# Two thirds of a mixture-of-experts stage sent through two experts by placed rows, the last block left as it was

## The chip, the core and the metric

The kernel runs on one core of a Trainium2 chip. The metric is the time of one execution in microseconds (us), a median over runs. The core has five engines that work side by side and are joined by semaphores: TensorE (PE in the profile; PEld is its weight load), VectorE (DVE), ScalarE (ACT), GpSimd (POOL) and SyncE (SP), which here only issues DMAs.

## The reference

A gated cross attention is followed by a mixture of experts. 1024 rows x of 128 values attend to 6404 context rows of 96 values. Then each row gets eight router weights, of which the two greatest are kept and scaled to sum to one, and eight experts (128 to 512, ReLU, 512 to 128) are summed with these weights.

```
x = x + tanh(g_xattn[0]) * xattn(layernorm(x), ctx_768, Wq, bq, Wk, bk, Wv, bv)
...
logits = einsum('bsd,de->bse', input_emb, Wr) + br          # input_emb = layernorm(x)
route_w = softmax(logits)
_, topk_idx = top_k(route_w, 2)
mask = one_hot(topk_idx, 8).sum(-2)
routed = route_w * mask
routed = routed / routed.sum(axis=-1, keepdims=True)
h = relu(einsum('bsd,edh->ebsh', input_emb, W1) + b1)
expert_out = einsum('ebsh,ehd->ebsd', h, W2) + b2
out = x + tanh(g_ffn[0]) * einsum('bse,ebsd->bsd', routed, expert_out)
```

For six of the eight experts a row's weight is zero, so what they make of it is multiplied by zero.

## The kernel before

All products that decide the result are made from a rounded value and its remainder (names ending in _hi and _lo): hi by hi, hi by lo and lo by hi, three matmuls for one product.

**Attention.** The rows are cut into tiles of 128 and into NB = 3 blocks of 2, 3 and 3 tiles. For each block a loop runs over UNITS = 26 units of two context chunks of 128 keys. In a unit TensorE makes the scores (`scores`, L943 to L945, six matmuls of 384 columns), ScalarE the exponentials, twice (L580 and L581), VectorE the remainder `ex_lo` (L751), and TensorE, LAG = 2 units later, the sum over values (`values`, L965 to L967). Score banks and remainders are in rings, so each engine is at most about two units ahead.

**What follows a block** (`post`) is spread over units of the next block by a table of unit numbers, POST_ATTENTION for blocks 0 and 1 and POST_EXPERTS for block 2: project, gate, residual, statistics (VectorE), normalisation (GpSimd, L392 and L399), transposes, router logits, comparison of the eight logits with each other (L704 to L713), weights. Every engine takes its own part of a step when its loop comes to the unit.

**Weights.** During block 2 the eight experts' weights are brought in by SP, rounded by VectorE (`round_weights`, L734 and L735) at units 6, 9, 11, 14, 17, 19, 22 and 25, and their remainders are made by GpSimd (L470 and L472, which tell TensorE by `w_lo_ready`). They are put where the context was, so each has to wait until the units that read the context there are done.

**Experts.** Two spans of four tiles (512 rows) go one after the other through all eight experts: 2 x 32 units, FU = 32 a span, each of three matmuls that make 128 hidden values of 512 rows (`hidden`, L1011 to L1013) and, H_LAG = 3 units later, three that add them to the output (`expert_out`, L1040 to L1042). ScalarE applies bias and ReLU twice (L597 and L598), VectorE makes the remainder (L795) and, once for each expert, scales the output by the router weights (`scale_output`, L776), which SP fetches spread over all partitions (L359); GpSimd adds (L465). `hidden` of expert e waits for that expert's weights alone.

The first two units of the experts are issued beside the last two `values` of the attention (`v` from 78 on in TensorE's outer loop). On each engine the order is that of the program.

## Time and profile before

| | us |
|---|---|
| three runs | 299.65, 297.44, 299.83 |
| median | 299.65 |
| the profiled execution, its own time | 298.64 |
| its span, first to last instruction | 296.7 |
| what lies around the span | 1.9 |
| granted TensorE clock, mean | 0.993 |

The profile is of one execution. Its page gives each engine's busy time, the span in 40 slices, the chain of work that ended last, and groups of instructions. The trace behind it can be asked for a stretch, for one line of the kernel, or for the instructions in order of time. TensorE's matmuls overlap each other: the time that one of them costs in a stream is the distance from its start to the next one's, not its duration.

### The profile page before, as it was taken

How to read it: one execution, taken by the hardware profiler on the slowest of the kernel's cores; microseconds unless marked ns; L12 is line 12 of the kernel's file. 1: busy time of each engine (PE TensorE's matmuls, PEld its weight loads, DVE VectorE, ACT ScalarE, POOL GpSimd, SP SyncE). 2: the span in 40 equal slices, each digit the busy share in tenths (PEclk: the TensorE clock that was granted, in tenths of full speed). 3: DMA queues.
4: the chain of work that ended last, by engine and by line, in shares of the span. 5: the costliest groups of instructions: out<-in, count | busy, mean ns of one | idle time of the engine just before them, and what ended most of it. 6: DMA issues, size and time to landing. Idle time of an engine off the chain costs nothing.

```text
span 296.7 us, 4637 instructions
## 1 busy us (share of the span) xinstructions
PE 287.5 (97%) x1595; PEld 252.1 (85%) x1595; DVE 218.7 (74%) x385; ACT 206.0 (69%) x337; POOL 86.7 (29%) x92
## 2 busy tenths in 40 slices
PE   7988999999999999999999999999999999999995
PEld 7657899999999999997999999888888878888883
DVE  5894989998788878895348867755858956666666
ACT  3981665556565665665776867669898888888881
POOL 3894998000000300000003963342332212111310
PEclk9997999999999999999999999999999999999999
DMA  6600022900000000000000220002111111221111
GB/s 209 220 2 0 1 62 86 282 0 2 0 2 0 0 3 0 0 3 1 0 2 0 71 74 0 0 4 71 36 38 35 61 48 38 60 82 36 52 56 35
DMA packets 10643, 12.41 MB, mean 42 GB/s; under 512 B 1531, under 2 KB 6525, under 8 KB 10621
## 3 DMA queue, kind: packets, MB, share of 16 engines
q1 hardware_dynamic: 10140, 11.90, 12.8%
q8 instruction: 13, 0.21, 0.3%
q10 hardware_dynamic: 480, 0.23, 0.3%
q14 instruction: 10, 0.07, 0.1%
HBM read 11.57 MB, written 0.56 MB: 41 GB/s over the span
## 4 chain that ended last, share of the span: by engine, by line
PE 89%; DVE 7%; issue 2%; ACT 1%; POOL 0%; ACTq 0%; DVEq 0%; POOLq 0%
PE ps L965 8%; PE ps L943 8%; PE ps L967 8%; PE ps L966 8%; PE ps L944 7%; PE ps L945 7%; PE ps L879 7%; PE ps L1011 5%; PE ps L1013 5%; PE ps L1041 5%; PE ps L1012 5%; PE ps L1042 5%; PE ps L1040 5%; DVE pmax L635 5%; PE ps L827 2%
## 5 line engine op out<-in xcount | busy, mean ns | idle before, releaser
L580 ACT ACTIVATE ex_hi<-ps 128x768 fp32r<-128x768 f32 (+1 forms) x78 | 56.9, 730 | 67.1 <-PE ps L945 66.9
L751 DVE TENSOR_TENSOR ex_lo<-ps,ex_hi 128x768 fp32r<-128x768 f32 (+1 forms) x78 | 66.4, 851 | 29.6 <-ACT ps L581 28.7
L635 DVE TENSOR_REDUCE pmax<-ps 128x1 f32<-128x512 f32 (+2 forms) x92 | 63.7, 731 | 6.8 <-PE ps L879 5.9
L795 DVE TENSOR_TENSOR ex_lo<-ps,ex_hi 128x512 fp32r<-128x512 f32 x64 | 44.1, 690 | 30.1 <-ACT ps L598 29.4
L581 ACT ACTIVATE ps<-ps 128x768 f32<-128x768 f32 (+1 forms) x78 | 56.6, 725 | 0.0
L597 ACT ACTIVATE ex_hi<-ps,cols 128x512 fp32r<-128x512 f32 x64 | 44.2, 691 | 11.3 <-PE ps L1013 10.7
L943 PE MATMUL ps<-q_hi,ctxT_hi 97*128 97x384 f32 (+1 forms) x153 | 49.9, 326 | 0.4 <-DVE ex_lo L751 0.2
L965 PE MATMUL ps<-ex_hi,ctx_hi 128*97 128x384 f32 (+1 forms) x153 | 49.5, 324 | 0.0
L944 PE MATMUL ps<-q_lo,ctxT_hi 96*128 96x384 f32 (+1 forms) x153 | 48.8, 319 | 0.0
L945 PE MATMUL ps<-q_hi,ctxT_lo 96*128 96x384 f32 (+1 forms) x153 | 48.8, 319 | 0.0
L966 PE MATMUL ps<-ex_hi,ctx_lo 128*96 128x384 f32 (+1 forms) x153 | 48.7, 318 | 0.0
L967 PE MATMUL ps<-ex_lo,ctx_hi 128*97 128x384 f32 (+1 forms) x153 | 48.7, 318 | 0.0
L598 ACT ACTIVATE ps<-ps,cols 128x512 f32<-128x512 f32 x64 | 41.9, 654 | 0.0
L392 POOL TENSOR_TENSOR rstd<-veps,minus_half 128x3 f32<-128x3 f32 (+1 forms) x6 | 4.9, 824 | 125.3 <-DVE veps L622 125.3
L879 PE MATMUL ps<-ctxT_hi,q_hi 97*128 97x512 f32 (+1 forms) x104 | 35.3, 408 | 2.8 <-DVE pmax L635 2.3
L465 POOL TENSOR_TENSOR acc<-acc,y_r 128x512 f32<-128x512 f32 x12 | 15.8, 1315 | 55.4 <-DVE y_r L776 55.4
L943 PEld LDWEIGHTS ps<-q_hi,ctxT_hi 97*128 97x128 f32 x153 | 28.7, 188 | 2.5 <-DVE ex_lo L751 1.5
L944 PEld LDWEIGHTS ps<-q_lo,ctxT_hi 96*128 96x128 f32 x153 | 29.2, 191 | 0.1
L945 PEld LDWEIGHTS ps<-q_hi,ctxT_lo 96*128 96x128 f32 x153 | 29.2, 191 | 0.0
L966 PEld LDWEIGHTS ps<-ex_hi,ctx_lo 128*96 128x96 f32 x153 | 24.8, 162 | 3.7
L965 PEld LDWEIGHTS ps<-ex_hi,ctx_hi 128*97 128x97 f32 x153 | 24.9, 163 | 2.4 <-issue 0.4
L967 PEld LDWEIGHTS ps<-ex_lo,ctx_hi 128*97 128x97 f32 x153 | 24.8, 162 | 1.4
...
## 6 DMA issues: line engine op xcount, KB each, us to landing
r_b<-routing SPq DMA_DIRECT2D x16, 256.0 KB, 3.2
...
w_raw<-in_L_ffn_W_dram SPq DMA_DIRECT2D x8, 256.0 KB, 3.1
raw<-in_L_ffn_W_dram SPq DMA_DIRECT2D x8, 256.0 KB, 4.4
...
out_dram<-norm SPq DMA_DIRECT2D x1, 256.0 KB, 2.8
tok<-in_x_dram SPq DMA_DIRECT2D x1, 128.0 KB, 2.3
out_dram<-norm SPq DMA_DIRECT2D x1, 128.0 KB, 1.7
```

The lines of the kernel that those rows point to most:

```text
L580: nc.scalar.activation(ex_pair(ex_hi, u % P_RING, js, n), scores, ACT.Exp)
L581: nc.scalar.activation(scores, scores, ACT.Exp).then_inc(ex_ready, 1)
L597: nc.scalar.activation(hid(ex_hi, u), src, ACT.Relu, bias=cols[:, i:i + 1])
L635: nc.vector.tensor_reduce(pmax[:, FIRST_TILE[b] + t, place:place + 1], max_home(s)[:, 0:w], AX.X, ALU.max).then_inc(max_reduced, 1)
L751: nc.vector.tensor_tensor(ex_pair(ex_lo, u % P_RING, js, n), whole, ex_pair(ex_hi, u % P_RING, js, n).bitcast(F32), ALU.subtract).then_inc ...
L879: last = nc.tensor.matmul(max_home(s)[:, at:at + n], q_hi[:, ft * P:(ft + 1) * P], ctxT_hi[0:CA, key + at:key + at + n], start=True, stop= ...
L943: nc.tensor.matmul(dst, ctxT_hi[0:CA, keys], q_hi[:, span(b)], start=True, stop=False)
L944: nc.tensor.matmul(dst, ctxT_hi[0:C, keys], q_lo[:, span(b)], start=False, stop=False)
L945: last = nc.tensor.matmul(dst, ctxT_lo[0:C, keys], q_hi[0:C, span(b)], start=False, stop=True)
L965: nc.tensor.matmul(dst[0:CA, 0:n], ch[:, j, :], hi, start=(j == 0), stop=False)
L966: nc.tensor.matmul(dst[0:C, 0:n], cl[:, j, :], hi, start=False, stop=False)
L967: last = nc.tensor.matmul(dst[0:CA, 0:n], ch[:, j, :], lo, start=False, stop=(j == NC - 1))
```

## The change

The rows of blocks 0 and 1 (PLACED = 5 tiles, 640 rows) are no longer taken through all experts. For each row and each of its two experts a slot number is worked out, such that the rows of an expert stand together and every expert begins at a multiple of 128. SLOT_TILES = 17 tiles of 128 slots are enough in every case, and all 17 are always worked through. GpSimd writes each normalised row to its two slots in memory by indirect DMAs (`place_rows`, one for each tile and choice, ten in all). SP loads the slot tiles back one by one. Each is taken through one expert, whose number is read from a table into a register (`load_columns`) and used as an address. The results are stored by slot and fetched by ten more indirect DMAs, and VectorE adds them, scaled, to the rows (`gather_sum`). The rows of block 2 (3 tiles, 384 rows) go through all eight experts as before, in 32 units that are 384 columns wide in place of 512.

The table POST_ATTENTION becomes POST_FIRST for block 0 and POST_PLACED for block 1, with new steps. The steps of block 2 are spread over the slot tiles (POST_LAST).

```diff
+POST_PLACED = dict(u_copy=2, project=3, gate=3, residual=4, stats=4, turn=7, logits=8, shift=8, compare=9, exp=9,
+                   rank=10, choose=10, weights=11, count=12, offsets=12, pick=13, tiles=13, slots=14, share=15, gains=16)
+POST_LAST = dict(u_copy=1, project=2, gate=2, residual=3, stats=3, turn=6, split=6, logits=7, shift=7, compare=8, exp=8,
+                 rank=9, weights=10, pick=10, share=11, turn_r=12, copy_r=12)
+TOP = 2
+LOAD_GROUP = 4
+PLACE_BEHIND = 4
+STORE_LAG = 6
+FIRST_SLOTS = [23, 25]
+GATHER_UNIT = 22
+def load_columns(nc, engine, row, last):
+    return list(nc.values_load_multi_w_load_instructions(row, engines=[engine], min_val=0, max_val=last)[1])
...
+    PLACED = FIRST_TILE[-1]
+    SLOT_TILES = (TOP * PLACED * P + E * (P - 1)) // P
+    SPAN_TILES = BLOCK_TILES[-1]
...
 SP:
+            for pair in range(E // 2):
+                sync.wait_ge(w_lo_ready, W_RING + pair + 1)
+                for e in range(2 * pair, 2 * pair + 2):
+                    row = b1[e:e + 1, :].partition_broadcast(P).rearrange("p a n -> p (a n)")
+                    sync.dma_start(bias_1[:, e * H:(e + 1) * H], row).then_inc(bias_1_in, 16)
+            def load_slots(j):
+                if j == 0:
+                    sync.wait_ge(rows_placed, 16 * TOP * PLACED)
+                if j >= X_RING:
+                    sync.wait_ge(xs_turned, j - X_RING + 1)
+                sync.dma_start(xs[:, j % X_RING, :], x_slots[j * P:(j + 1) * P, :]).then_inc(xs_in[j % X_RING], 16)
...
 GpSimd:
+            def place_rows(t):
+                for k in range(TOP):
+                    nc.gpsimd.indirect_dma_start(x_slots[:, :], bass.IndirectOffsetOnAxis(ap=slot[:, k, t:t + 1], axis=0),
+                                                 norm[:, t, :], None).then_inc(rows_placed, 16)
+            for e in range(PLACE_BEHIND):
+                split_weights(e)
+            pool.wait_ge(slots_ready, 1)
+            pool.wait_ge(zeroes_in, 16)
+            pool.wait_ge(norm_ready, 2 * NB - 2)
+            for t in range(PLACED):
+                place_rows(t)
+            for e in range(PLACE_BEHIND, E):
+                split_weights(e)
...
+            def sum_slots(j):
+                if j % LOAD_GROUP == 0:
+                    columns[:] = load_columns(nc, mybir.EngineType.Pool, column_of[0:1, 1, j:j + LOAD_GROUP], (E - 1) * P)
+                at = columns[j % LOAD_GROUP]
+                pool.wait_ge(ys_copied, j + 1)
+                half = ys[:, j % Y_RING, 0, :]
+                step(nc.gpsimd.tensor_tensor(half, half, ys[:, j % Y_RING, 1, :], ALU.add))
+                nc.gpsimd.tensor_tensor(half, half, bias_2[:, bass.ds(at, P)], ALU.add).then_inc(ys_summed, 1)
...
 VectorE:
-                        if b == NB - 1 and i == min(split_unit(e) + LAG + 2, UNITS - 1):
+                        if b == NB - 1 and i == min(split_unit(e) + LAG + 2, UNITS - 2):
                             round_weights(e)
...
+            for v in range(SLOT_TILES + 1):
+                if v < SLOT_TILES:
+                    if v == 0:
+                        dve.wait_ge(columns_ready, 1)
+                        dve.wait_ge(w_lo_ready, E)
+                        dve.wait_ge(bias_1_in, 16 * E)
+                    if v % LOAD_GROUP == 0:
+                        columns[:] = load_columns(nc, mybir.EngineType.DVE, column_of[0:1, 0, v:v + LOAD_GROUP], (E - 1) * H)
+                    dve.wait_ge(hs_made, v + 1)
...
+                    nc.vector.tensor_tensor(h_sum[:, v % 2, :], hs_bank(v)[:, 0:H],
+                                            bias_1[:, bass.ds(columns[v % LOAD_GROUP], H)], ALU.add).then_inc(hs_summed, 1)
+                if v + 2 < SLOT_TILES:
+                    split_slots(v + 2)
+                if v >= 1:
+                    j = v - 1
+                    dve.wait_ge(hs_hi_ready, j + 1)
+                    nc.vector.scalar_tensor_tensor(out=hsT(ex_lo, j), in0=hsT_bank(j)[:, 0:H], scalar=0.0,
+                                                   in1=hsT(ex_hi, j).bitcast(F32), op0=ALU.max,
+                                                   op1=ALU.subtract).then_inc(hs_lo_ready, 1)
+                if v < SLOT_TILES:
+                    post(NB - 1, v)
...
+                if u == GATHER_UNIT:
+                    gather_sum()
...
 TensorE:
+            def turn_slots(j):
+                pe.wait_ge(xs_in[j % X_RING], 16 * (j // X_RING + 1))
...
+                nc.tensor.transpose(XS_BANK, xs[:, j % X_RING, :], ident[:, :]).then_inc(xs_turned, 1)
+            def slot_hidden(j):
+                at = columns[j // LOAD_GROUP % 2][j % LOAD_GROUP]
+                pe.wait_ge(xs_lo_ready, j + 1)
+                if j == 0:
+                    pe.wait_ge(w_lo_ready, E)
...
+                nc.tensor.matmul(dst, xs_hi[:, j % 2, :], w1_hi[:, bass.ds(at, H)], start=True, stop=False)
+                nc.tensor.matmul(dst, xs_hi[:, j % 2, :], w1_lo[:, bass.ds(at, H)], start=False, stop=False)
+                nc.tensor.matmul(dst, xs_lo[:, j % 2, :], w1_hi[:, bass.ds(at, H)], start=False, stop=True).then_inc(hs_made, 1)
+            def slot_output(j):
...
+                for c in range(HC):
...
+                    nc.tensor.matmul(dst, hi, from_c[:, :, bass.ds(at, P)], start=(c == 0), stop=False)
+                    last = nc.tensor.matmul(dst[:, 0, :], lo, from_c[:, 0, bass.ds(at, P)], start=False, stop=(c == HC - 1))
+            def slot_tile(v):
+                if v < SLOT_TILES:
+                    slot_hidden(v)
+                if v + 2 < SLOT_TILES:
+                    turn_slots(v + 2)
+                if 1 <= v <= SLOT_TILES:
+                    turn_slot_hidden(v - 1)
+                if (v + 1) % LOAD_GROUP == 0 and v + 1 < SLOT_TILES:
+                    slot_columns(v + 1)
...
+                    if b == NB - 1:
+                        for j, unit in enumerate(FIRST_SLOTS):
+                            if i == unit:
+                                turn_slots(j)
+                        if i == FIRST_SLOTS[0] + 1:
+                            pe.wait_ge(columns_ready, 1)
+                            slot_columns(0)
```

**Place 1: GpSimd, from the sixth expert's weights to the experts' stage.** Before, the remainders of the weights (ctxT_lo and ctx_lo take them) stand directly ahead of the last normalisation and the twelve additions:

```order
L470 TENSOR_TENSOR ctxT_lo<-w_raw,ctxT_hi 128x512
L472 TENSOR_TENSOR ctx_lo<-w_raw,ctx_hi 128x512
L392 TENSOR_TENSOR rstd<-veps,minus_half 128x3
L399 TENSOR_SCALAR norm<-tok,mv,rstd 128x128 x3
L465 TENSOR_TENSOR acc<-acc,y_r 128x512 x12
```

Now, from the fourth expert's weights on:

```order
L584 TENSOR_TENSOR ctxT_lo<-raw,ctxT_hi 128x512
L586 TENSOR_TENSOR ctx_both<-raw,ctx_both 128x512
L593 DMA x_slots<-norm,slot 2176x128 x10
L584 TENSOR_TENSOR ctxT_lo<-raw,ctxT_hi 128x512
L586 TENSOR_TENSOR ctx_both<-raw,ctx_both 128x512
```

and where the weights end and the slot tiles' sums begin:

```order
L584 TENSOR_TENSOR ctxT_lo<-w_raw,ctxT_hi 128x512
L586 TENSOR_TENSOR ctx_both<-w_raw,ctx_both 128x512
L73 TENSOR_LOAD column_of
L73 ISA x8
L615 TENSOR_TENSOR shared<-shared 128x128
L616 ISA
L616 TENSOR_TENSOR shared<-shared 128x128
L501 TENSOR_TENSOR rstd<-veps,minus_half 128x3
```

The ten indirect DMAs stand between the weights of the fourth and the fifth expert; the remainders of experts four to seven (counted from zero) come behind them.

**Place 2: TensorE, the end of the last block of attention and the start of the experts.** Before, the first unit of the experts follows the last scores:

```order
L943 MATMUL ps<-q_hi,ctxT_hi 128x384 [waits lo_ready]
L944 MATMUL ps<-q_lo,ctxT_hi 128x384
L945 MATMUL ps<-q_hi,ctxT_lo 128x384
L965 MATMUL ps<-ex_hi,ctx_hi 97x384 [waits lo_ready]
L966 MATMUL ps<-ex_hi,ctx_lo 96x384
L967 MATMUL ps<-ex_lo,ctx_hi 97x384
```

Now, behind the scores of unit 23, the transpose of the first slot tile, and the first unit of the slots waits for all weights:

```order
L1209 MATMUL ps<-q_hi,ctxT_lo 128x384
L1275 MATMUL ps<-ident,shared 128x128 [waits slots_ready,xs_in0]
L1229 MATMUL ps<-ex_hi,ctx_both 97x384 [waits lo_ready]
...
L1209 MATMUL ps<-q_hi,ctxT_lo 128x384
L73 TENSOR_LOAD column_of [waits columns_ready]
L73 ISA x8
L1229 MATMUL ps<-ex_hi,ctx_both 97x384 [waits lo_ready]
...
L1291 ISA [waits lo_ready,w_lo_ready,xs_lo_ready]
L1291 MATMUL ps<-ctxT_hi,xs_hi 128x512
```

Everything that TensorE still has to do for block 2 now stands behind the arrival of slot tile 0.

**Place 3: VectorE, a slot tile with steps of block 2 behind it.** Before, a unit of the experts is one instruction, with one more for each expert:

```order
L795 TENSOR_TENSOR ex_lo<-ps,ex_hi 128x512 [waits h_ready] x4
L795 TENSOR_TENSOR ex_lo<-ps,ex_hi 128x512 [waits h_used,h_ready] x2
L675 RECIPROCAL rsum<-ps 128x3 [waits projected]
L677 TENSOR_SCALAR gsum<-rsum,tanh_g 128x3 [waits tanh_ready,dve_step]
```

Now tile 3 (the bias is added, the slot tile of two tiles later split, the remainder of the tile before made):

```order
L1015 ISA
L1015 TENSOR_TENSOR w_raw<-ps,raw 128x512
L969 TENSOR_TENSOR xs_lo<-ps,xs_hi 128x128
L1022 SCALAR_TENSOR_TENSOR ex_lo<-ps,ex_hi 128x512
L867 SCALAR_TENSOR_TENSOR tok<-ps,gsum,tok 128x128 x3
L803 BN_STATS stats<-tok 128x6 x3
L806 BN_AGGR mv<-stats 128x2 x3
L808 TENSOR_SCALAR veps<-mv 128x3
L73 TENSOR_LOAD column_of
L73 ISA x8
```

Where there was one long instruction for each unit there are three for each tile, and the steps of block 2 stand behind them in the same queue.

## Rows read from the trace of the kernel before

**Rows 1.** The page: span and busy time of the engines.

```profile
span 296.7 us, 4637 instructions
PE 287.5 (97%) x1595; PEld 252.1 (85%) x1595; DVE 218.7 (74%) x385; ACT 206.0 (69%) x337; POOL 86.7 (29%) x92
```

**Rows 2.** Busy time by stretch: PE, PEld, DVE, ACT, POOL, clock, DMA share, GB/s.

```profile
20.00:30.00 10.00, 8.55 (x44) 6.43 (x44) 6.19 (x15) 2.53 (x7) 6.17 (x7) 0.83 0.00 0
...
200.00:290.00 90.00, 90.00 (x403) 72.92 (x402) 60.35 (x107) 79.18 (x132) 20.81 (x18) 1.00 0.16 50
290.00:297.00 7.00, 3.25 (x17) 2.08 (x15) 3.87 (x8) 0.04 (x1) 0.00 (x0) 0.92 0.11 37
```

**Rows 3.** One line, L1011: duration min/median/max, first and last start.

```profile
L1011 PE MATMUL ps<-xT_hi,ctxT_hi x64: 388/398/399, 197.9 to 287.9; 128*128 128x512 f32 x64
```

**Rows 4.** PE in order of time, matmuls of 512, 384, 256, 128 and 8 columns.

```profile
249.94 0.39 PE L1012 MATMUL ps<-xT_lo,ctxT_hi 128*128 128x512 f32 x1
250.17 0.40 PE L1013 MATMUL ps<-xT_hi,ctxT_lo 128*128 128x512 f32 x1
...
191.03 0.34 PE L943 MATMUL ps<-q_hi,ctxT_hi 97*128 97x384 f32 x1
191.21 0.34 PE L944 MATMUL ps<-q_lo,ctxT_hi 96*128 96x384 f32 x1
...
30.73 0.28 PE L945 MATMUL ps<-q_hi,ctxT_lo 96*128 96x256 f32 x1
30.85 0.28 PE L943 MATMUL ps<-q_hi,ctxT_hi 97*128 97x256 f32 x1
...
14.83 1.04 PE L846 MATMUL ps<-ident,raw 128*96 128x128 f32 x8
15.62 0.71 PE L879 MATMUL ps<-ctxT_hi,q_hi 97*128 97x512 f32 x2
...
172.05 0.73 PE L986 MATMUL ps<-wr_sb,xT 128*128 128x8 f32 x6
172.64 0.39 PE L965 MATMUL ps<-ex_hi,ctx_hi 128*97 128x384 f32 x1
```

**Rows 5.** POOL in order of time, remainders of the weights.

```profile
176.75 1.29 POOL L472 TENSOR_TENSOR ctx_lo<-raw,ctx_hi 128x512 fp32r<-128x512 f32 x1
```

**Rows 6.** VectorE in order of time, the last units of block 2.

```profile
195.95 0.96 DVE L751 TENSOR_TENSOR ex_lo<-ps,ex_hi 128x768 fp32r<-128x768 f32 x1 [1.05 <-ACT ps L581]
...
198.42 0.42 DVE L734 CAST ctxT_hi<-w_raw 128x512 fp32r<-128x512 f32 x1
```

**Rows 7.** Groups by line and shape: busy us, mean ns, idle before.

```profile
L598 ACT ACTIVATE ps<-ps,cols 128x512 f32<-128x512 f32 x64 | 41.9, 654 | 0.0
L580 ACT ACTIVATE ex_hi<-ps 128x768 fp32r<-128x768 f32 x50 | 40.6, 812 | 41.3 <-PE ps L945 41.2
L795 DVE TENSOR_TENSOR ex_lo<-ps,ex_hi 128x512 fp32r<-128x512 f32 x64 | 44.1, 690 | 30.1 <-ACT ps L598 29.4 <-DVE cmp_eq L705 0.2
L776 DVE SCALAR_TENSOR_TENSOR y_r<-ps,cols,r_b 128x512 f32<-128x512 f32 x13 | 9.6, 742 | 0.0
L751 DVE TENSOR_TENSOR ex_lo<-ps,ex_hi 128x384 fp32r<-128x384 f32 x2 | 1.1, 558 | 1.1 <-ACT ps L581 1.0
L681 DVE SCALAR_TENSOR_TENSOR tok<-ps,gsum,tok 128x128 f32<-128x128 f32 x8 | 2.3, 341 | 0.0
L711 DVE TENSOR_TENSOR cmp_gt<-cmp_gt,cmp_eq 128x192 f32<-128x192 f32 x2 | 1.7, 846 | 0.1
L717 DVE RECIPROCAL einv<-esum 128x3 f32<-128x3 f32 x2 | 0.4, 178 | 0.1
```

**Rows 8.** The page, DMA issues: KB each, median us from issue to landing.

```profile
r_b<-routing SPq DMA_DIRECT2D x16, 256.0 KB, 3.2
...
tok<-in_x_dram SPq DMA_DIRECT2D x1, 128.0 KB, 2.3
```

**Rows 9.** The issue of one DMA on ScalarE's queue.

```profile
198.33 0.28 ACTq L568 DMA_DIRECT2D routing<-rT  x1
```

550 lines of the change are left out of this document (374 added, 176 removed).

## The prediction

> **What bounds the kernel now.** I read the page first: TensorE is busy 97% of the span, VectorE 74%, ScalarE 69%, GpSimd 29% [rows 1]. Then the busy time by stretch: in the expert stage, 200 to 290 us, TensorE has no gap, ScalarE is at 79 of 90 us, VectorE at 60, GpSimd at 21, and the clock is whole [rows 2]. Then the line of the first matmul of a unit: 64 units begin between 197.9 and 287.9 [rows 3], so one takes some 1.4 us. Last the order in time: in a stream a 512-column matmul costs 0.234 us, a 384-column one 0.175, a 256-column one 0.12, a transpose 0.10 (eight in 0.79), and even with 8 columns it is 0.098 (six in 0.59) [rows 4]. The stage is bound by TensorE's columns, 64 x 6 x 0.234 = 89.9 us, and fewer columns shorten it as long as nothing else becomes the limit.
>
> **What TensorE saves.** The 89.9 us go. A slot tile has three matmuls of 512 columns (0.70), one transpose of the rows and four of the hidden values (0.50), four of 256 columns and four of 128 (4 x 0.22 = 0.88): 2.08 us, and 17 tiles make 35.4. The last block has 32 x 6 matmuls of 384 columns, 33.6. Together 69.0, so 20.9 us are saved. A 128-column matmul of rounded values is not in the trace; between 0.06 (half of a 256-column one) and 0.12, I take 0.10, the transpose's, since the 8-column rows show that nothing shorter is had.
>
> **What is given back at the start.** Before, TensorE goes from the last scores into the experts with one expert's weights made. Now three things stand in a row. (1) The slots are known in unit 14, once the fourth expert's weights are rounded, so GpSimd starts on the ten indirect DMAs when that expert's remainders end, 176.75 + 1.29 = 178.0 [rows 5]. No DMA issued by GpSimd is in the trace. An issue on ScalarE's queue is 0.28 [rows 9] and a whole 128 KB load from issue to landing 2.3 [rows 8]; between them I take 1.0, near the work of one instruction on this engine over a wide tile (1.29), since a list of 128 addresses has to be made: 10 us, to 188.0. (2) Experts four and five follow, 4 x 1.29, to 193.2. SP has waited for expert five to send the last two biases, and the load of slot tile 0 stands behind them: three issues and a landing of 2.3 bring it to about 196. TensorE wants it behind the scores of unit 23, which begin at 191.03 [rows 4] and take 1.05: at 192.1. It stands for 3.9 us, with scores 24 and 25 and the values behind it, and ScalarE and VectorE run dry. (3) The first slot tile waits for all eight experts. The eighth is rounded behind the remainder of unit 24. From 196.1: values 1.05, scores 1.05, hand-over, two exponentials of 0.81, remainder 0.96, two casts of 0.42 [rows 6, 7], GpSimd 2.6: 204.6 in place of 197.9, **+6.7**. Were slot tile 0 there in time, the eighth expert alone would give 195.95 + 0.96 + 0.84 + 2.6 = 200.4, +2.5: the lower bound. At 2.0 for each DMA it is +16.7, the upper. Each 0.1 us costs 1.0.
>
> The Trainium skill, "DMA: Bandwidth & Descriptors", section on the anatomy of a DMA on GpSimd's path, has a fixed cost of about 2.0 us per DMA, most of it a wait for the write that later DMAs can pass; were it paid ten times over, the start would be at the upper bound.
>
> **Registers.** TensorE loads four column numbers every fourth tile, four times within the loop: a load and eight register instructions. Two instructions of a pair are issued in 0.098 us [rows 4], so eight are 0.4, and the load I put at the smallest read that any engine does, 0.18 [rows 7]: 0.6 each, **+2.4**. Below, the queue ahead of TensorE hides them (0); above, each is a memory's round trip of 2.3: +9.2. The waits for VectorE around them leave no long queue, so I take them as bare. Operands whose address is in a register, and some six register instructions in each tile, I put at nothing, since they can be issued while earlier matmuls run (2.08 us of matmuls for about forty instructions is 0.05 for each, just the issue rate of the 8-column row). That cover is thin: at 0.5 us a tile it would be +8.5.
>
> **VectorE.** A tile takes 0.69 for the bias (like L795), some 0.3 for the rows' remainder (L681 is 0.34), 0.74 for the hidden remainder: 1.73 of TensorE's 2.08, so 0.35 are free in a tile [rows 7]. The steps of block 2, which ran hidden under the old stage (60 of 90 us busy), are now spread over tiles 2 to 11: three of 0.34 and their like, the comparisons with one of 0.85, and a dozen of 0.18, with hand-overs some 8 us. 3.5 fit, **+4.5**. Bounds: +2 (the steps in which VectorE waits anyway), and +9 where VectorE stands in its own queue for TensorE's transpose and ScalarE's copies at tile 6 while the bias of tile 7 is due. The 26 small operations that work out the slots (26 x 0.2) lie in block 2, where VectorE waits 1.05 us before a unit's remainder [rows 6]; nothing, at most +2.
>
> **Filling and changing over.** The first tiles have no output to do beside them, and the first four units of the last block wait for banks that tiles leave: **+1.5** (0.5 to 3), from two chains of TensorE, ScalarE, VectorE of some 2.3 us that overlap in part.
>
> **The last block.** ScalarE's two ReLUs of 384 columns: 0.65 at 512, less 128 columns at 0.84 ns (0.812 us for 768 columns, about 0.60 for 512), 0.55 each and overlapped; below the 1.05 of TensorE. In unit 22 VectorE does the ten sums of `gather_sum`, 10 x 0.34 = 3.4. A remainder is needed three units after its scores, and is there after 2.3 us of 3.7: 1.4 hide, **+2.0** (0 to 6, the upper if the fetched rows are late: ten indirect DMAs again, on the same engine).
>
> **Sum.** -20.9 + 6.7 + 2.4 + 4.5 + 1.5 + 2.0 = -3.8: a span of 292.9, with the 1.9 around it 294.8. The profiled execution (298.64) lies 1.0 below the median (299.65) and 1.2 above the lowest; I put the median of the changed kernel half of that higher, **295.3 us**.
>
> **Rivals.**
> *Slower: GpSimd's queue.* If an indirect DMA holds GpSimd for 1.8 us, slot tile 0 lands 8 us later, and TensorE stands before unit 24 for 12 us. For it: the DMAs stand in front of four experts' remainders [rows 5], and one engine makes all lists. Against it: GpSimd has 7 us free in this stretch. Price: +8.0, 303.3; against the run before it decides from 1.4 us a DMA. The Trainium skill, "SBUF — State Buffer", on its two sides, says that a DMA issued by GpSimd makes its descriptors through ports that some VectorE copies lock; six casts of 0.42 lie in the stretch, so by the page at most 2.5 us more. A cast beside GpSimd's subtractions is not slower in the rows shown.
> *Slower: the issue of instructions.* The slot tile's period is not 2.08 but 2.6: 303.8. For it: forty instructions, six of them on registers. Against: nothing in the trace, which has no address in a register.
> *Faster: the waits are covered.* DMAs of 0.5 us or less: start +2.5, register loads 0, VectorE +2.5, filling and sums +2: -13.9, 286. For it: the old stage left VectorE 30 us and GpSimd 69 us idle.
> *Even: the clock.* TensorE stands twice for some 4 us at the start. In the stretch 20 to 30 us, in which it was busy for 8.55 us after waits, the granted clock was 0.83, a mix of 2.4 and 1.2 GHz [rows 2]. One such stretch costs 1.7 us, two 3.4: 298.7. The Trainium skill, "TensorE: Matmul & The Clock Gate", part 1, says that an idle engine falls to half its clock; that agrees with the row.
> That the change doesn't do what it says: the number of tiles is fixed at 17 and doesn't follow the data, so TensorE's saving stands for every routing.
>
> **How the numbers follow.** A difference under about 1% can't be told from none here. Chances: the forecast, 290 to 299, 0.42; GpSimd's queue 0.22; the issue rate 0.12; covered 0.18; the clock 0.06. Of the forecast's 0.42 some 0.31 lies more than 1% below 299.65, under 296.65. Faster 0.31 + 0.18 = 0.49; within 1% 0.11 + 0.06 + 0.02 of the mild ends of the first two rivals = 0.19; slower 0.32. The range has to reach the covered case and most of the first two rivals: 284 to 307.
>
> **What would show it.** Behind the scores of unit 23 TensorE waits for the load of a slot tile for 2 to 6 us, and the first slot tile begins at 203 to 207. Tiles follow each other at 2.1 us, at 2.5 to 3 where steps of block 2 lie, and at 2.7 where registers are loaded. The last block's units come at 1.05 us with one gap of about 2 behind unit 22. The indirect DMAs' length on GpSimd decides more than anything else: over 1.4 us and the forecast is wrong. A tile period over 2.4 without steps of block 2 would mean the issue of instructions.

## The result, and the profile after

The changed kernel takes 312.47 us (median of 4 runs, 311.56 to 314.38), the kernel before 298.54 (4 runs, 297.12 to 299.83) on the same chip: ratio 1.048, 95% interval 1.040 to 1.056. It is slower by 4.8%, where 295.3 us was forecast and the range ended at 307. The profiled execution took 311.56 us. Its span and busy times, for [rows 1]:

```profile
span 309.8 us, 5195 instructions
PE 277.6 (90%) x1667; PEld 251.8 (81%) x1667; DVE 219.9 (71%) x429; ACT 178.9 (58%) x320; POOL 111.9 (36%) x149
```

TensorE is busy for 90% of a longer span, where it was 97%. The time is no longer set by its columns alone. Busy time by stretch, around the new stage (columns as in [rows 2]):

```profile
200.00:210.00 10.00, 3.51 (x15) 2.99 (x14) 3.87 (x5) 2.19 (x4) 5.01 (x5) 0.71 0.42 131
210.00:220.00 10.00, 6.75 (x30) 5.79 (x30) 3.02 (x7) 2.85 (x6) 2.48 (x2) 0.84 0.03 8
220.00:230.00 10.00, 10.00 (x70) 9.13 (x69) 6.85 (x19) 4.61 (x11) 0.91 (x2) 0.93 0.09 26
230.00:240.00 10.00, 5.76 (x38) 4.80 (x36) 5.05 (x13) 2.77 (x7) 5.86 (x10) 0.92 0.15 43
240.00:250.00 10.00, 9.78 (x65) 8.42 (x64) 6.48 (x16) 5.04 (x14) 3.40 (x8) 0.91 0.14 39
```

The first number behind the length is TensorE's busy time. TensorE stands for 6.5 and 3.2 of the microseconds from 200 to 220, which the prediction knew of, and for 4.2 of those from 230 to 240, which it did not. The clock is 0.71 and 0.84, where from 200 to 290 it had been whole [rows 2]. What TensorE waited for, in order of time (start, length, engine, line; in brackets the idle time before it and what ended it):

```profile
158.37 0.55 PE L1119 MATMUL ps<-ident,norm 128*128 128x128 f32 x3 [1.45 <-POOL norm L508]
199.75 0.34 PE L1207 MATMUL ps<-q_hi,ctxT_hi 97*128 97x384 f32 x1
207.47 0.48 PE L1275 MATMUL ps<-ident,shared 128*128 128x128 f32 x1 [6.49 <-DMA shared<-x_slots]
217.51 0.49 PE L1291 MATMUL ps<-ctxT_hi,xs_hi 128*128 x1 [3.25 <-POOL ctx_both L586]
233.00 0.30 PE L1275 MATMUL ps<-ident,shared 128*128 128x128 f32 x1 [2.17 <-DVE xs_lo L969]
237.50 0.33 PE L1275 MATMUL ps<-ident,shared 128*128 128x128 f32 x1 [2.07 <-DMA shared<-x_slots]
```

The second row opens the scores of unit 23 of block 2. Before they began at 191.03 [rows 4], now at 199.75: **most of the loss has already happened when the new stage comes.** Slot tile 0's load is waited for at 207.47, the eighth expert's remainder at 217.51, the first slot tile, which was forecast for 204.6.

The span falls into four parts that every run below has: block 2 from the scores of its unit 0 to those of unit 23 (140.30 to 191.03 before, 139.84 to 199.75 after), from there to the first slot tile or expert ("start"), the slot stage up to the last block's first hidden unit (266.19), and the last block with the tail. In microseconds:

| | before | forecast | after |
|---|---|---|---|
| block 2, units 0 to 23 | 50.7 | 50.7 | 59.9 |
| start | 6.9 | 13.6 | 17.8 |
| slot stage | (old stage) | 43.8 | 48.7 |
| last block and tail | (old stage) | 44.5 | 43.6 |

The misses are +9.2, +4.2, +4.9 and -0.9; block 2 also begins 0.5 earlier. Together 16.9, the whole way from the forecast span, 292.9, to 309.8.

GpSimd at the start, for [rows 5]:

```profile
184.84 1.24 POOL L593 DMA_INDIRECT x_slots<-norm,slot  x1 [0.88 <-DVE slot L951]
196.53 0.96 POOL L593 DMA_INDIRECT x_slots<-norm,slot  x1 [0.30 <-issue]
```

The first and the tenth indirect DMA: 0.96 us each and 0.30 between two, 1.26 where 1.0 was taken. The first starts at 184.84, not at 178.0, because the slots come late. Each lands 2.2 us after its issue (median), but the next one does not wait for that, so the start is not at the prediction's upper bound of 2.0 a DMA.

### The profile page after: what moved, and what is told of

Read it like the earlier page. It is cut to its first block, busy times and chain, and to the rows that moved or that the text cites. A ratio compares the mean times of both kernels' runs of the same rounds, so it can differ in the third digit from the quotient of the medians.

```text
span 309.8 us, 5195 instructions
## 1 busy us (share of the span) xinstructions
PE 277.6 (90%) x1667; PEld 251.8 (81%) x1667; DVE 219.9 (71%) x429; ACT 178.9 (58%) x320; POOL 111.9 (36%) x149
## 4 chain that ended last, share of the span: by engine, by line
PE 70%; DVE 14%; issue 5%; POOL 4%; DMA 2%; ACT 2%; SPq 1%; POOLq 0%; DVEq 0%; ACTq 0%
PE ps L1229 7%; PE ps L1207 7%; PE ps L1230 7%; PE ps L1231 7%; PE ps L1208 7%; PE ps L1209 7%; PE ps L1143 6%; DVE pmax L821 4%; PE ps L1314 3%; PE ps L1302 2%; DVE ex_lo L985 2%; DMA raw<-in_ctx_dram 2%; PE ps L1377 2%; POOL norm L508 2%; PE ps L1339 2%
## 5 line engine op out<-in xcount | busy, mean ns | idle before, releaser
L1207 PE MATMUL ps<-q_hi,ctxT_hi 97*128 97x384 f32 (+1 forms) x153 | 50.8, 332 | 4.5 <-DVE ex_lo L985 4.4
L1229 PE MATMUL ps<-ex_hi,ctx_both 128*97 128x384 f32 (+1 forms) x153 | 50.9, 333 | 0.0
L1230 PE MATMUL ps<-ex_hi,ctx_both 128*96 128x384 f32 (+1 forms) x153 | 49.7, 325 | 0.0
L1231 PE MATMUL ps<-ex_lo,ctx_both 128*97 128x384 f32 (+1 forms) x153 | 49.6, 324 | 0.0
L1230 PEld LDWEIGHTS ps<-ex_hi,ctx_both 128*96 128x96 f32 x153 | 25.5, 167 | 3.7
L1229 PEld LDWEIGHTS ps<-ex_hi,ctx_both 128*97 128x97 f32 x153 | 25.6, 167 | 2.5 <-issue 0.7
L1231 PEld LDWEIGHTS ps<-ex_lo,ctx_both 128*97 128x97 f32 x153 | 25.5, 167 | 1.5
L1064 DVE TENSOR_TENSOR ex_lo<-ps,ex_hi 128x384 fp32r<-128x384 f32 x32 | 17.6, 557 | 12.2 <-ACT ps L786 12.2
L1143 PEld LDWEIGHTS ps<-ctxT_hi,q_hi 97*128 97x128 f32 x104 | 17.7, 190 | 6.5 <-DVE pmax L821 5.4
L1015 DVE TENSOR_TENSOR w_raw<-ps,raw 128x512 f32<-128x512 f32 x17 | 11.7, 691 | 13.1 <-PE ps L1293 8.7
L785 ACT ACTIVATE ex_hi<-ps,cols 128x384 fp32r<-128x384 f32 x32 | 19.4, 607 | 1.5 <-PE ps L1341 1.0
```

What stands on the lines that cost most here:

```text
L785: nc.scalar.activation(hid(ex_hi, u), src, ACT.Relu, bias=cols[:, u:u + 1])
L1143: last = nc.tensor.matmul(max_home(s)[:, at:at + n], q_hi[:, ft * P:(ft + 1) * P], ctxT_hi[0:CA, key + at:key + at + n], start=True, stop= ...
L1207: nc.tensor.matmul(dst, ctxT_hi[0:CA, keys], q_hi[:, span(b)], start=True, stop=False)
L1229: nc.tensor.matmul(dst[0:CA, 0:n], ch[:, j, :], hi, start=(j == 0), stop=False)
L1230: nc.tensor.matmul(dst[0:C, 0:n], cl[:, j, :], hi, start=False, stop=False)
L1231: last = nc.tensor.matmul(dst[0:CA, 0:n], ch[:, j, :], lo, start=False, stop=(j == NC - 1))
```

## Experiments

Three theories stood against each other. **Steps:** block 2 lost its 9 us in VectorE's queue (earlier steps, 26 small operations, a port shared with GpSimd). **Queues:** GpSimd's and SyncE's orders make the stalls. **Columns:** the saving itself is not there. Some edits were timed on different chips; they are called A (first four runs), B (next four) and C (the last eight), and C was timed in two groups of four. Medians of the kernel before were 297.52 (A), 299.06 (B), 297.50 and 299.06 (C, first and second group). It has two levels, near 297.4 and near 299.6, on every chip, and its median moves with their mix. So differences of less than 2 us between kernels of different groups tell nothing, and the changed kernel itself was not timed on chip A.

### Block 2: earlier steps, small operations, and the port

First the old kernel with one table of the change:

```
-            return (POST_ATTENTION if b < NB - 1 else POST_EXPERTS)[name] == i
+            return [POST_ATTENTION, POST_SECOND, POST_EXPERTS][b][name] == i   # turn 12 -> 7, shift 15 -> 8, share 23 -> 15
```

> The kernel before, with the steps of block 1 behind its attention at the units that the change gives them (project at 3, turn at 7, logits and shift at 8, share at 15) and nothing else. Theory 'earlier steps': units 0 to 23 of block 2 take 51 us or more instead of 48.6, TensorE waits 1 to 2 us for GpSimd's normalisation at unit 7, and the time is 2 to 4 us above the kernel before. Theory 'small operations': block 2 takes 48.5 to 50 us and the time is within 1.5 us of the kernel before.

Measured (chip A): 301.29 us, ratio 1.012 (1.004 to 1.019), 3.8 us more; block 2's units 0 to 23 take 54.37, 3.6 more. Unit 8 alone takes 4.2 us; at the turn TensorE waits 1.47 us for GpSimd's normalisation, as after. (The expectations of this and the next run count 57.8 and 48.6 from unit 1, not 0; the differences are the same.) The earlier steps alone cost 3.6 us in block 2, and the rest of its 9.2, 5.5 us, needs something more. Next, the changed kernel without the tables:

```
-                   rank=10, choose=10, weights=11, count=12, offsets=12, pick=13, tiles=13, slots=14, share=15, gains=16)
+                   rank=10, weights=11, pick=13, share=15)
...
+            nc.gpsimd.iota(slot[:, :, :], [[P, TOP * PLACED]], base=0, channel_multiplier=1).then_inc(slots_ready, 1)
```

> Left out: the counting of the rows by expert and everything worked out from it (choose, count, offsets, tiles, slots, gains). Slots, the experts of the slot tiles and the gains are constants that GpSimd writes early, so the output is another one; every transfer and every matmul of the slot stage stays. Theory 'small operations' (the some 26 additional VectorE operations inside block 2's attention cost most of its 9 us): units 0 to 23 of block 2 take 49 to 51 us, not 57.8 (before 48.6), and the time falls by 6 to 9 us to 304 to 306. Rival 'earlier steps' (the old steps, closer together and with the turn at unit 7, cost it): block 2 stays above 55 us and the time above 309. Rival 'GpSimd's queue': the placing DMAs can start as soon as GpSimd has done expert 3's remainder, TensorE's stall for slot tile 0 stays above 4 us whatever block 2 does.

Measured (A): block 2 takes 54.13 us, as in the run above. Yet the time is 317.03 us, ratio 1.063 (1.055 to 1.071): TensorE then stands 9.7 us for slot tile 0, since nothing at the start has become earlier than GpSimd's and SyncE's queues allow (that rival was right), and 7 us go in the last block to something new (below). The first slot tile starts at 213.35, 4.2 us earlier than in the changed kernel. That the additional operations are needed for the long block 2 is confirmed, the forecast of the time is not.

```
-PLACE_BEHIND = 4
+PLACE_BEHIND = 0
```

> GpSimd computes no weight remainder before the rows are placed, so that none of its subtractions runs beside VectorE's small operations of block 1. Theory 'shared port': the four operations that took 1.1 to 1.5 us (comparison for equality, the product with the inverse sum, two of the slot operations) take 0.2 to 0.4 us, block 2's units 0 to 23 take 55.5 to 56.5 us instead of 59.9, and the slots are ready 3 to 4 us earlier. Rival 'long by themselves': they keep their length, and block 2 stays at 59 to 60. The eight remainders then stand behind the DMAs, 20 us together, so the first slot tile starts at 216 to 221 whatever block 2 does.

Measured (B, a single run, so the time has no interval): 318.82 us. The first slot tile starts at 222.52, later still than expected, behind the eight remainders. Block 2 takes 54.50 us instead of 59.91. The four VectorE operations, first in the changed kernel:

```profile
167.16 1.45 DVE L891 TENSOR_TENSOR cmp_eq<-lg 128x192 f32<-128x192 f32 x1
173.01 1.07 DVE L904 TENSOR_TENSOR le<-le,einv 128x24 f32<-128x24 f32 x1
181.51 1.28 DVE L946 SCALAR_TENSOR_TENSOR place<-first_of,place 128x40 f32<-128x40 f32 x1
182.82 1.24 DVE L948 TENSOR_TENSOR picked_place<-chosen,place 128x80 f32<-128x80 f32 x1
```

and here, where GpSimd subtracts nothing meanwhile:

```profile
165.88 0.35 DVE L891 TENSOR_TENSOR cmp_eq<-lg 128x192 f32<-128x192 f32 x1
170.54 0.18 DVE L904 TENSOR_TENSOR le<-le,einv 128x24 f32<-128x24 f32 x1
178.40 0.20 DVE L946 SCALAR_TENSOR_TENSOR place<-first_of,place 128x40 f32<-128x40 f32 x1
178.64 0.24 DVE L948 TENSOR_TENSOR picked_place<-chosen,place 128x80 f32<-128x80 f32 x1
```

5.04 us against 0.97. GpSimd's two subtractions in the changed kernel that the third and fourth row meet:

```profile
181.45 1.28 POOL L584 TENSOR_TENSOR ctxT_lo<-raw,ctxT_hi 128x512 fp32r<-128x512 f32 x1 [6.15 <-DVE ctx_both L964]
182.69 1.27 POOL L586 TENSOR_TENSOR ctx_both<-raw,ctx_both 128x512 fp32r<-128x512 f32 x1
```

The third and the fourth VectorE row end at 182.79 and 184.06, GpSimd's at 182.73 and 183.96: the operation lasts until the subtraction is over. The Trainium skill, "SBUF — State Buffer", section on the two separate sides, says that VectorE and GpSimd take turns at one port pair, the whole instruction long, when a VectorE operation has two inputs in SBUF and GpSimd reads SBUF; these rows agree, at 0.9 to 1.1 us a meeting. So the four meetings are 4.1 of the 5.4 us that block 2 gets back. The split of its 9.2 us is then: 5.4 with the meetings, 3.8 with the earlier steps and the small operations together. How the 3.8 divide is known only roughly: the old kernel with the earlier steps alone, which has the first two of the meetings (1.45 and 1.06 us, 2.0 too long), takes 54.37, and the changed kernel with all small operations and no meeting 54.50, so the small operations by themselves cost between 0.1 and some 2 us, as forecast. Next, the rows placed earlier, on top of three edits that are told further down:

```
-PLACE_BEHIND = 4
+PLACE_BEHIND = 2
```

> The kernel with three edits, with the rows placed behind the remainder of expert 1 instead of expert 3. Theory 'shared port': fewer of VectorE's small operations meet a subtraction of GpSimd, block 2's units 0 to 23 take 54.5 to 56 us instead of 57.9, the placing starts 2 to 3 us earlier, the first slot tile starts at 208 to 210 us although GpSimd has five us more behind the placing, and the time falls by 1 to 3 us to 300 to 302. Rival 'GpSimd's queue': the first slot tile moves to 212 to 215 us, and the time rises by 1 to 4 us.

Measured (C): 310.68 us, ratio 1.045 (1.037 to 1.053); block 2 takes 53.59 us instead of 57.91 (57.91 also in a trace of chip C that has the same block 2, the run without register loads below), and the placing starts at 180.47 instead of 184.88. Both are as the port theory had it. But what block 2 gains the start takes back: the first slot tile starts at 211.09, against 210.91 without this edit on chip B and 209.30 in that trace of chip C, neither the 208 to 210 of the theory nor the 212 to 215 of the rival. The time is 2.1 us below the 312.74 of the same kernel without this edit on chip C, but that was timed in the other group, and the ratios to the kernel before, 1.045 and 1.043, don't differ. No gain in time is shown, and the forecast of 300 to 302 is wrong.

### The start and the slot stage: two queues

```
+            for pair in range(BIAS_AHEAD): fetch_bias(pair)             # BIAS_AHEAD = 2
             for j in range(SLOT_TILES + STORE_LAG):
+                if j == X_RING - 1:
+                    for pair in range(BIAS_AHEAD, E // 2): fetch_bias(pair)
                 if j < SLOT_TILES: load_slots(j)
```

> SyncE issues the first two loads of slot tiles ahead of the last two pairs of bias rows, where they stand behind the rows' arrival alone (about 199.7 us) and not behind the remainder of expert 5 (202.5 us) and four transfers of 256 KB. Theory 'SyncE's queue': slot tile 0 lands at 201.5 to 202.5, TensorE's stall falls from 6.5 us to 0.5 to 1.5, the clock does not fall there, the first slot tile starts at 210 to 213 instead of 217.5, and the time falls by 5 to 7 us to 305.5 to 307.5. Rival 'weights': the stall goes over to the wait for the remainder of expert 7, which grows from 3.3 us to more than 6, and the time falls by less than 3 us.

Measured (A): 313.76 us, ratio 1.051 (1.045 to 1.058). TensorE no longer waits for slot tile 0 (6.5 us before), the wait for the eighth expert stays at 3.26 (so the rival is out), and the first slot tile starts at 213.56 instead of 217.51. But a new wait of 3.4 us for VectorE stands at unit 23, and the last block loses 8.3 in this trace, which is of the longest of its five runs (318.20). The wait at unit 23 does not come from the edit. ScalarE stood 4.2 us ahead of it, for something that no instruction near it ended:

```profile
199.95 0.81 ACT L753 ACTIVATE ex_hi<-ps 128x768 fp32r<-128x768 f32 x1 [4.22 <-remote]
```

The next run, with another edit, also has a wait there (1.98 us). The step is right; what it is worth in time this chip does not tell (see "What chips A and C add").

```
-            sum_slots(0)
+            for j in range(3): sum_slots(j)
             inverse_deviation(2 * NB - 1); normalize(2 * NB - 1)
-            for j in range(1, SLOT_TILES): sum_slots(j)
+            for j in range(3, SLOT_TILES): sum_slots(j)
```

> GpSimd normalises block 2 behind the sum of slot tile 2 instead of slot tile 0, so that the stores of tiles 1 and 2 and the loads behind them on SyncE's queue are not held. Theory 'second stall': the wait for a slot tile's load (2.1 us near 237) goes, the tiles 6 to 8 take 2.2 to 2.8 us each instead of 4.6, 5.5 and 3.7, and the time falls by 2.5 to 5 us to 307.5 to 310. Rival 'VectorE': the tiles wait for VectorE's remainders of the slot tiles, behind block 2's steps and the register loads; then two of the three tiles stay above 4 us, and the time falls by less than 1.5 us.

The chain it aims at, in the changed kernel's trace, GpSimd first, then SyncE's queue:

```profile
230.51 0.88 POOL L501 TENSOR_TENSOR rstd<-veps,minus_half 128x3 f32<-128x3 f32 x1 [3.87 <-DVE veps L808]
231.51 2.36 POOL L508 TENSOR_SCALAR norm<-tok,mv,rstd 128x128 f32<-128x128 f32 x3
233.84 0.45 POOL L615 TENSOR_TENSOR shared<-shared 128x128 f32<-128x128 f32 x1
...
234.95 0.32 SPq L462 DMA_DIRECT2D y_slots<-shared  x1
235.31 0.64 SPq L458 DMA_DIRECT2D shared<-x_slots  x1
```

GpSimd stands 3.87 us for block 2's variances with tile 1 waiting to be summed behind them; the store of tile 1 goes out at 234.95, the load behind it at 235.31, and TensorE has been waiting for that load (the row at 237.50 above). Measured (A): 314.84 us, ratio 1.055 (1.048 to 1.063), above the 307.5 to 310 of the forecast. But the slot stage is 44.9 us instead of 48.7, and the tile that took 5.45 us takes 2.43. Again the last block is 6.6 us longer, and block 2 takes 62.0. What three traces of chip A share came in question, first by the changed kernel once more, with no edit:

> The changed kernel once more, with nothing edited. In three edited kernels TensorE's semaphore updates stood still for 1.5 to 5 us and then came 0.1 us apart, once near the end of the ten indirect DMAs that place the rows and once near the end of the ten that fetch them; the first trace of the changed kernel has neither. Theory 'held updates come and go': this execution shows at least one of the two (a wait of ScalarE of 4 to 5 us near 280 to 287 us that nothing in the profile ends), and its span is 2 to 6 us above 309.8. Rival 'it hangs on the edit': neither is there, and the span is within 1.5 us of 309.8.

Measured (B): 311.73 us, ratio 1.041 (1.036 to 1.046); no late update, last block 36.0. The theory as put (it comes and goes between executions) fell. The stages are 58.4, 19.4, 50.8 and 43.6: so one trace's stage is known to 1.5 or 2 us, and 44.9 stands apart from 48.7 and 50.8. All traces bear this out: with the order of before the slot stage takes 48.7 to 51.0 in seven, with the sums first and the register loads in place 44.9 to 46.4 in five. Both edits together, and a third, which turns the first slot tiles and does block 1's steps one unit later:

```
-FIRST_SLOTS = [23, 25]
+FIRST_SLOTS = [24, 25]
...
-turn=7, logits=8, shift=8, compare=9, ... slots=14, share=15, gains=16
+turn=8, logits=9, shift=9, compare=10, ... slots=15, share=16, gains=17
```

> The loads of the slot tiles ahead of the last bias rows, block 2's normalisation behind the third sum, the first slot tiles turned at units 24 and 25, and every step of block 1 from its turn on one unit later (turn at 8, slots at 15). Theory 'each stall has its own cause': block 2's units 0 to 23 take 57.5 to 58.5 us, the first slot tile starts at 210 to 212 us, the slot stage has no stall above 2 us, and the span is 299 to 303 us, 2 to 4 us more with held updates; so the kernel is still not faster than the one before. Rival 'one resource behind all': what is taken from one wait comes back in the next, as in the two single edits, and the span stays above 308 us.

Measured (B): 302.84 us, ratio to the kernel before 1.014 (1.009 to 1.019), 8.9 us less than the changed kernel on that chip. Block 2 takes 57.9, the first slot tile starts at 210.9, the slot stage takes 46.0. Against the changed kernel's trace on chip B the first slot tile is 6.9 us earlier and the slot stage 4.8 shorter. The single edits had given 4.0 and 3.7 on chip A, so what is taken from one wait does not come back in the next. (The third edit was not run by itself.) One stall of 2.8 us in block 2 and one of 2.2 in the slot stage are above the forecast. It is still slower than the kernel before, by 1.4%.

Two runs price terms of the sum. Without the indirect DMAs:

```
-                    nc.gpsimd.indirect_dma_start(x_slots[:, :], ...)      # ten of them, and the ten of the gather
+                pass
```

> Left out: both sets of ten indirect DMAs. No row is placed, so the slot tiles hold zeros, and the rows summed at the end are whatever lies in the tile; all tables, loads, stores and matmuls stay. Theory 'held updates are the indirect DMAs': no late update of TensorE anywhere; the stall ahead of the first slot tile is 6 to 9 us shorter in all, because GpSimd's queue holds 12.6 us less, and the last block has no gap above 1.2 us besides the sum; the time falls by 9 to 14 us to 299 to 303. Rival 'they are incidental': TensorE's updates are still late near 280 to 290, and the time falls by 5 us at most.

Measured (B): 306.27 us, ratio 1.028 (1.021 to 1.036), 5.5 us below the changed kernel, not 9 to 14. The first slot tile starts 6.7 us earlier (211.07 against 217.78); then it waits for the eighth expert, which VectorE rounds only behind unit 24. The last block does not change (36.0), so the gather is hidden on this chip. Since chip B has no late update with the DMAs either, the run does not tell where these come from. Without the loads of registers, on top of the three edits:

```
-    return list(nc.values_load_multi_w_load_instructions(row, engines=[engine], min_val=0, max_val=last)[1])
+    return [0] * LOAD_GROUP
```

> The kernel with three edits, but the loads of registers on TensorE, VectorE and GpSimd are left out and every slot tile goes through expert 0, so the output is another one; the tables are still computed and the rows placed. The prediction put the registers at 2.4 us (8.5 at most). Theory 'as predicted': the slot stage takes 43 to 44 us instead of 46.0, and the time falls by 2 to 3 us. Rival 'they hide behind VectorE's steps': under 1 us. Rival 'operands in registers slow the matmuls': the undisturbed tile falls from 2.18 us to 2.08 or less, and the stage to 41 or less.

Measured (C): 307.11 us, ratio 1.031 (1.024 to 1.037), 5.6 below the three edits on chip C (of the other group; by the ratios 1.2%, 3.6 us); the slot stage takes 41.3 us against 46.4 there and 46.0 on chip B. So the loads cost 4.7 to 5.1 against these two traces, and 3.6 to 3.9 against the two that have the sums first alone (44.9 and 45.2, where the stall at tile 7 is gone too): by one trace each, one and a half times to twice the 2.4 of the forecast. Neither a hidden load nor a slow operand, the two rivals, is what the trace has: the loads stand in three queues, and VectorE's hold the bias that TensorE waits for. In the changed kernel VectorE idles ahead of tile 4's bias for nothing but its load:

```profile
231.96 0.69 DVE L1015 TENSOR_TENSOR w_raw<-ps,raw 128x512 f32<-128x512 f32 x1 [1.53 <-issue]
```

That is 1.5 us for a load of four registers, where 0.6 was taken: the load itself takes 0.34 (0.18 was taken), and each of the four numbers an instruction of 0.18 and a shorter one behind it (0.05 for each was taken). The undisturbed tile is 2.17 to 2.19 us with and without them: operands in registers cost nothing.

### What chips A and C add

The kernel with the sums first, once more and with no edit:

> The kernel of the earlier experiment once more, with nothing edited (block 2's normalisation behind the third sum). Its first trace lost 6.6 us in the last block to late updates of TensorE, its slot stage took 44.9 us where the changed kernel's took 48.7 and 50.8. Theory 'held updates belong to the execution or the chip': this trace has none, the last block takes 36.0 us again, and the median falls from 314.8 to 305.5 to 307.5 us. Rival 'they belong to the program': the gap near hidden unit 16 is back at 4 to 5 us, and the median stays at 313 to 316.

Measured (C): 313.78 us, ratio 1.052 (1.045 to 1.060). The slot stage is 45.2, a confirmation, and the loss near hidden unit 16 is back. Taken alone this speaks for the program. But all kernels with indirect DMAs so far lost time in the last block on A and C and none on B, so chip and program had to be told apart, with the changed kernel and the three edits, unedited, on chip C:

> The changed kernel, nothing edited. Theory 'it hangs on the chip': where the ten indirect DMAs in the kernel before show late updates, this kernel shows them twice and measures 316 to 320 us; where they don't, none and 310 to 313.5 us. Rival 'it hangs on the program': none here, whatever the others show.

> The kernel with three edits once more. Theory 'it hangs on the chip': 308 to 312 us with late updates in the two runs beside it, 302 to 304 without. Rival 'it hangs on the program': 302 to 304 on either.

Measured: the changed kernel 318.23 us, ratio 1.064 (1.058 to 1.069), against 311.73 on B; the three edits 312.74, ratio 1.043 (1.035 to 1.050), against 302.84 on B. It hangs on the chip, not the program. The changed kernel is now the measure on chip C for the single edit of GpSimd's order: 318.23 without it, 313.78 with it (1.064 and 1.052 times the kernel before, in different groups, 3.4 us by the ratios). So that edit does gain, within its forecast of 2.5 to 5, and the 314.84 of chip A was read against a chip without late updates. The changed kernel on chip C, last block, ScalarE and then GpSimd's last DMA:

```profile
282.27 0.55 ACT L786 ACTIVATE ps<-ps,cols 128x384 f32<-128x384 f32 x1
285.35 0.58 ACT L785 ACTIVATE ex_hi<-ps,cols 128x384 fp32r<-128x384 f32 x1 [2.54 <-PE ps L1341]
287.54 0.58 ACT L785 ACTIVATE ex_hi<-ps,cols 128x384 fp32r<-128x384 f32 x1 [1.16 <-remote]
...
284.55 0.95 POOL L630 DMA_INDIRECT w_raw<-y_slots,slot  x1 [0.30 <-issue]
```

and TensorE, whose matmuls ScalarE is waiting for:

```profile
280.16 0.34 PE L1341 MATMUL ps<-xT_hi,ctxT_lo 128*128 128x384 f32 x1
281.20 0.34 PE L1341 MATMUL ps<-xT_hi,ctxT_lo 128*128 128x384 f32 x1
282.26 0.33 PE L1341 MATMUL ps<-xT_hi,ctxT_lo 128*128 128x384 f32 x1
284.44 0.33 PE L1341 MATMUL ps<-xT_hi,ctxT_lo 128*128 128x384 f32 x1
```

These end hidden units' groups, one each 1.05 us, and are recorded as over by 282.6. ScalarE gets its next one at 285.35. The trace's semaphore records show three updates of this kind at 287.5, 287.6 and 287.7, 0.1 us apart, though the groups were over 1 us and more apart. "Remote" in brackets says that no recorded instruction lies near enough to the update to be its cause. So updates were held, until 2 us behind the end of the tenth DMA. Whether TensorE's work stood or only its messages, the trace can't say, since its ends are modelled. The clock then pays too. Busy time and clock from 288 to 294 us on chip C:

```profile
288.00:294.00 6.00, 5.13 (x17) 4.81 (x17) 3.22 (x6) 4.97 (x12) 1.01 (x1) 0.53 0.10 34
```

and in the first trace of the same kernel:

```profile
288.00:294.00 6.00, 6.00 (x36) 6.00 (x35) 3.76 (x8) 5.86 (x13) 2.03 (x2) 1.00 0.22 62
```

0.53 is 1.2 GHz for nearly all of it and 2.4 for the rest, and units come at 1.92 instead of 1.05 us. The Trainium skill, "TensorE: Matmul & The Clock Gate", part 1, has the clock fall behind an idle engine; these rows agree. From its first to its last hidden unit the last block takes 42.5 to 44.3 us in all eight traces of kernels with the slot stage on chips A and C, and 36.0 in the four on B (one of them has no indirect DMA) and in the first comparison. Block 2 pays too: 62.9 in this trace, where it was 59.9 and 58.4 elsewhere. On chip A the old kernel with earlier steps, which has no indirect DMA, shows no late update. Then the same in the kernel before, ten DMAs behind the weights' remainders:

```
+            for t in range(10):
+                nc.gpsimd.indirect_dma_start(spare[:, :], bass.IndirectOffsetOnAxis(ap=at_row[:, t:t + 1], axis=0),
+                                             source[:, :], None).then_inc(rows_sent, 16)
```

> The kernel before, with ten indirect DMAs of 128 rows of 512 bytes added to GpSimd's queue behind the weights' remainders; they write constants to a tensor that nothing reads, so the output is the same. Theory 'held updates come with indirect DMAs, in some executions': if this trace shows late updates of TensorE, they lie within 2 us of the end of these DMAs; each DMA takes 0.96 us and 0.30 between two. If it shows none, the time is within 1 us of the kernel before, since GpSimd has room there: its next work is the first half's second expert. Rival 'the DMAs slow the others by themselves': matmuls or exponentials beside them take longer, and the time rises by 2 us or more with no late update.

Measured (C): 301.60 us, ratio 1.011 (1.005 to 1.017), 4.1 more, with late updates between 211.1 and 215.7 us; the tenth DMA ends at 213.56. The matmuls and exponentials beside the DMAs keep their length, so the rival is out. Once more beside its counterpart:

> The kernel before with ten indirect DMAs once more, beside the others on this chip: with late updates 3 to 4 us above the kernel before (301.6 against 297.5 measured), without them within 1 us of it.

```
-                nc.gpsimd.indirect_dma_start(spare[:, :], ...)
+                nc.gpsimd.dma_start(spare[t * P:(t + 1) * P, :], source[:, :]).then_inc(rows_sent, 16)
```

> The kernel before with ten plain DMAs of GpSimd in place of the ten indirect ones (128 rows of 512 bytes each, from the same tile to the same tensor that nothing reads). If the chip is one with late updates: theory 'any DMA that GpSimd's software issues': they are there again within 2 us of the end of the ten, and the time is 3 to 4 us above the kernel before. Rival 'indirect DMAs alone': none, and the time is within 1 us of the kernel before. On a chip without late updates in the run with indirect DMAs beside it, this run tells only the length of a plain DMA, 0.9 to 1.1 us.

Measured (C, ten runs each): 301.73 us with indirect DMAs, ratio 1.007 (1.004 to 1.011), 2.7 above the kernel before and so just under the forecast of 3 to 4, and 298.21 with plain ones, ratio 0.999 (0.995 to 1.003), no late update. The medians lie 3.5 apart, but both kernels have two levels, 299.9 and 301.8 with indirect DMAs, 297.4 and 299.4 with plain ones: level by level the difference is about 2.5. Indirect (ScalarE, then the tenth DMA and what follows it), then plain:

```profile
213.28 0.69 ACT L607 ACTIVATE ex_hi<-ps,cols 128x512 fp32r<-128x512 f32 x1 [1.17 <-PE ps L1023]
217.66 0.69 ACT L607 ACTIVATE ex_hi<-ps,cols 128x512 fp32r<-128x512 f32 x1 [3.14 <-PE ps L1023]
...
214.74 0.95 POOL L484 DMA_INDIRECT spare<-source,at_row  x1 [0.31 <-issue]
215.71 0.90 POOL L397 TENSOR_TENSOR rstd<-veps,minus_half 128x3 f32<-128x3 f32 x1
```

```profile
203.31 5.59 POOL L484 DMA_DIRECT2D spare<-source  x10 [0.31 <-POOL at_row L482]
```

The bytes, the rows and the engine that issues are the same; that the DMAs go by a list of addresses makes the difference. A plain DMA also comes every 0.56 us (0.54 of them busy), under the 0.9 to 1.1 expected and less than half of the 1.26 of an indirect one.

## Why the prediction was wrong, point by point

- **"The 26 small operations ... nothing, at most +2", and the steps of block 1 that move earlier, which have no term at all.** Here it failed: +9.2 us, more than the whole distance from the forecast to no change. 5.4 of them are gone when no small operation meets a subtraction of GpSimd (54.5), and 4.1 of these are the four operations' own lengthening. The other 3.8 come with the earlier steps, and in some part with the small operations; the old kernel with the earlier steps alone, two meetings included, lost 3.6. The price of one small operation, 0.2, was right; that it stands in an in-order queue beside another engine's 1.3 us was left out. The trace of before had shown it. L711 in [rows 7], two inputs in SBUF, has a mean of 846 ns over two executions, one in block 2 beside a subtraction and one in the experts' stage:

```profile
184.10 1.33 DVE L711 TENSOR_TENSOR cmp_gt<-cmp_gt,cmp_eq 128x192 f32<-128x192 f32 x1
230.79 0.36 DVE L711 TENSOR_TENSOR cmp_gt<-cmp_gt,cmp_eq 128x192 f32<-128x192 f32 x1
...
183.75 1.46 POOL L472 TENSOR_TENSOR ctx_lo<-raw,ctx_hi 128x512 fp32r<-128x512 f32 x1
```

The mean was read as its length ("one of 0.85"). The port was weighed for casts and descriptors alone, and the sentence that a cast beside GpSimd's subtractions is not slower has no row behind it: no row shown is such a cast, and in the same trace two casts beside subtractions, at 167.62 and 168.45, took 0.91 and 1.52 us instead of 0.42.
- **Start, "+6.7".** Measured 10.9 over the kernel before. The mechanism was right: the load of slot tile 0, then the eighth expert, in the order foreseen. Mis-sized: the DMA (1.26 us for 1.0, 2.6 us in all); what follows expert five until slot tile 0 is used, 4.9 us (202.53 to 207.47) instead of 2.8, since its load stands behind four transfers of 256 KB; and the clock: behind the stall some eleven matmuls follow each other at 0.32 us instead of 0.175, about 1.6 us, which had been put in a rival only. Against these 6.3 stand 1.9: unit 23 came 8.7 us later, the placing only 6.8, and that much of the wait fell away. That the late slots delay the placing is counted in block 2.
- **The rival "GpSimd's queue"** had the place right and decides from 1.4 us a DMA; at 1.26 it did not. The run without any indirect DMA is still 7.2 us above the kernel before, so the indirect DMAs in this queue are not the main cause.
- **Registers, "+2.4"**: 3.6 to 5.1, since a load costs VectorE 1.5 us and not 0.6. **Operands in registers, nothing**: right. **Tile of 2.08**: 2.18, so the saved columns are there less 1.7 us; the rival "issue of instructions", 2.6 a tile, is refuted.
- **VectorE "+4.5" and filling "+1.5"**: with the order of GpSimd's queue repaired the slot stage is 44.9 to 45.2, less 37.1 for seventeen tiles and 4.7 for registers leaves 3.3 for both (4.4 if registers are 3.6). The stall that was there instead, normalisation ahead of the second sum, store and load behind it, cost 3.7 to 5.9 (48.7 and 50.8 against 44.9 to 45.2) and had no term: the prediction spoke of VectorE at tile 6, and did not follow GpSimd and SyncE past the moved step.
- **The last block, "+2.0" for the sum of the fetched rows**: 1.0 (one unit of 2.04 us, the 27th, where others take 1.05), and the fetch is hidden, on a chip without late updates.
- The sum as made in the prediction, -3.8, with the measured sizes: -20.9 + 1.7 (tiles) + 9.2 - 0.5 (block 2) + 10.9 (start) + 4.7 (registers) + 3.3 (VectorE, filling) + 3.7 (second stall) + 1.0 (sums) = +13.1, the difference of the spans. It comes out exactly because the 3.3 and the 3.7 are what is left of the slot stage, not measurements of their own.
- In the rival "covered", -13.9 by the base of the sum (296.7 + 1.9 + 0.5) gives 285.2, not 286; nothing hangs on it.

**What stays open.** How the 3.8 us of block 2 that are not meetings divide between earlier steps and small operations was not separated, nor how much of the first two meetings' 2.0 us reaches TensorE. Why chips differ in the late updates, and whether chips A and C or chip B is the rule, three chips can't tell; the first trace's chip behaves like B. A version that beats the kernel before was not found. The run without register loads is 307.11 on C, where late updates cost the three edits 9.9 us against chip B; taken off, it would be about 297 by this estimate, level with the kernel before, and only if the loads were free.
